# Second edge stage of a four-layer graph kernel: softmax chain over seven steps, ring of 19 groups, neighbour table made once

## Chip, cores and metric
One NeuronCore of a Trainium2 chip. The metric is the device time of one execution in microseconds, as the median of several.

## The reference
Four graph layers, one after the other, on 3125 nodes of 64 features and 53125 edges (`src`, `dst`), sorted by `dst`; each layer adds to `x` what it makes of `h = relu(layernorm(x))`. The change is in the second, a graph attention layer with 4 heads of 64 features and a self-loop on each node:

```python
xw = (x @ W).reshape(n, H, C)                      # H = 4, C = 64
alpha = a_src_n[src2] + a_dst_n[dst2] + a_edge     # an edge and head each; src2, dst2 with self-loops
alpha = jnp.where(alpha >= 0, alpha, NEG_SLOPE * alpha)
amax = jax.ops.segment_max(alpha, dst2, num_segments=n)
ae = jnp.exp(alpha - amax[dst2])
attn = ae / jax.ops.segment_sum(ae, dst2, num_segments=n)[dst2]
agg = jax.ops.segment_sum(xw[src2] * attn[:, :, None], dst2, num_segments=n)
proj = (agg.reshape(n, H * C) + bias) @ Wp + bp     # then elu, a residual, a layer norm
```

## The kernel before, in words
Edges stand in 416 tiles of 128, the edge on the partition. Four tiles are a group (104 groups), eight groups a chunk of 32 tiles (13 chunks). The program is one block of instruction streams after another, all engines meeting between two blocks: setup, then for each layer a node block, an edge block and a fold.

**Setup** (L166 on). SyncE loads indices and weights, VectorE makes `dloc` and (L227) `dr_b`, each edge's place in the window of its tile, which goes to DRAM as `DL`.

**Node block of layer 2** (to L910). It makes a table `T1` in DRAM with one row of 324 numbers a node: 256 of `h @ W @ Wp`, 4 logits of the source, 64 of `h`. The 260 first also stay in SBUF as `ytab`, a view of the big accumulator's planes `acc[:, 1:3]` (125 partitions, 25 nodes in each); they are what the self-loops need later. SyncE stores them by seven DMAs (L836).

**Edge block of layer 2** (L977 to L1390), all unrolled, in steps x = 0, 1, ...; each engine goes through the same steps with its part:
- GpSimd gathers group g's rows of `T1` into a ring `ga` of RG = 14 groups by four indirect DMAs (L985); a group's room is free when TensorE has summed it (L982, L983).
- SyncE loads places `dl`, windows `win` of the destination table (24 bf16 columns, a number split in three) and, once a chunk, `drow`, the destinations in row form.
- ScalarE makes `oneT` (`places(x)`, L1019, L1021) and `one` (`one_hots`, L1028, L1032), copies loop weights (L1039), takes the exponents (L1044) and copies the finished weights of a chunk to SBUF (`back_on_edges`, L1052).
- TensorE: `logits(x)`, four matmuls of 24 columns (L1077) into one of two half banks; `sums` of group x - SCATTER (L1089, and L1098 for the node whose edges go over a chunk's end); small transposes and matmuls of the softmax.
- VectorE: the softmax of a chunk c, with its maxima and sums over equal destinations, first in rows of a transposed form (scans, L1242, L1243, ...), then over the 32 tiles (L1251 ...). `half_logits` (L1194) adds the three parts of four groups' logits; `logits(c)` at x % 8 = 0 (L1210 to L1217), `tops` also at 0 (L1235 to L1243, ends with L1222), `highest` (L1250 to L1261) and `sums_of_rows` (L1268 to L1270, L1222) at 1, `weights` (L1279 to L1294) and `carried` (L1300 to L1308) at 2, `hold` at 4 (L1313, L1314), `turn` at 5 (L1320), `settle` at 6 (L1328, L1330). In every step it also weighs a group, x - WEIGH with WEIGH = 11 (`weigh`: L1344, L1346, L1350), and adds the sums of group x - 12 to the accumulator at four starts read from memory into registers (`add_sums`: L1354, then L1360 four times).

`k.link` marks an instruction's end on a semaphore and lets the engine's next one wait for it; `k.mark` only marks it. The order of VectorE's step is written out by hand:

```python
if x % CG == 0 and soft: logits(c)
if x % CG == 1 and soft: highest(c)
if x % CG == 2 and soft: weights(c)
if 0 <= x - WEIGH < G:   weigh(x - WEIGH)
if x % CG == 0 and soft: tops(c)
if x % CG == 1 and soft: sums_of_rows(c)
if x % CG == 2 and soft: carried(c)
```

**Fold of layer 2** (L1403 on). In seven rounds of four nodes a partition: TensorE transposes the accumulator (L1410), VectorE adds (L1435, L1437), GpSimd multiplies `ytab` by the loops' weights (L1419), VectorE reduces it over the heads (L1429) and adds (L1430). Elu and layer norm follow when all rounds are done (L1444 on).

Of the kernel before, what the change touches and what calls it, by code (L numbers as in the profile page):

```python
# [92 lines left out]
def build(nc, A, out):  # L93
    with ExitStack() as ctx:
# [61 lines left out]
        DL = dram("DL", [1, EP], BF16)  # L156

# [3 lines left out]
        l_zero, l_d, l_dl = sem("l_zero"), sem("l_d"), sem("l_dl")  # L161
# [3 lines left out]
        dr_b = tmp("dr_b", [NT // GT, GT, W], BF16)  # L165
        with nc.Block() as block:  # L166
            @block.sync
            def _(sp):
# [18 lines left out]
                sp.dma_start(wre[REL:REL + 16, D:D + 4], v16[:]).then_inc(l_dl, 16)  # L187
                sp.wait_ge(l_dl, 32)
# [20 lines left out]
            def _(dve):  # L209
# [17 lines left out]
                c.mark(dve.tensor_tensor(dr_b[:], dr_f[:], dr_f[:, :, 0:1].to_broadcast([NT // GT, GT, W]), ALU.subtract))  # L227

# [171 lines left out]
        with nc.Block() as block:  # L400
# [21 lines left out]
            def _(act):  # L422
# [9 lines left out]
                act.wait_ge(e0_ones, 2)  # L432
                each_group(act, messages)
# [376 lines left out]
        with nc.Block() as block:  # L810
# [76 lines left out]
            def _(pe):  # L887
# [27 lines left out]
        G = NT // GT  # L915
        CT = 32
        CG = CT // GT
        NC = NT // CT
        RG = 14
        WEIGH = CG + 3  # L920
# [7 lines left out]
         e1_rv, e1_rh, e1_ab, e1_B, e1_ex, e1_wy, e1_ms, e1_ml, e1_S, e1_spec, e1_fix, e1_fold, e1_half, e1_exs, e1_hT, e1_own, e1_acc) = [  # L928
            sem("e1_" + x) for x in
            ("rows", "set", "oa", "one", "ta", "oT", "P", "c", "al", "T", "top", "r1", "x", "e", "f0", "sum", "r2",  # L930
             "rv", "rh", "ab", "B", "ex", "wy", "ms", "ml", "S", "spec", "fix", "fold", "half", "exs", "hT", "own", "acc")]
        HALF = CT // 2
        ga = tmp("ga1", [128, RG * GT, GW])
# [9 lines left out]
        drow = tmp("drow", [128, 2, 128], I32)  # L943
        same = tmp("same", [128, 129])
        gap = tmp("gap", [128, 129])
# [4 lines left out]
        lgt = tmp("lgt", [128, 8, CT])  # L950
# [21 lines left out]
        ring = lambda g: g % RG * GT  # L972
# [4 lines left out]
        with nc.Block() as block:  # L977
            @block.gpsimd
            def _(pool):
                for g in range(G):  # L980
# [3 lines left out]
                    for t in range(GT):  # L984
                        pool.indirect_dma_start(ga[:, ring(g) + t, :], None, T1, bass.IndirectOffsetOnAxis(  # L985
                            ap=src_i[:, g * GT + t:g * GT + t + 1], axis=0)).then_inc(e1_g[g % RG], 16)
# [26 lines left out]
            def _(act):  # L1013
# [39 lines left out]

                act.wait_ge(e1_set, 2)
                for x in range(G + SCATTER + 1):
# [3 lines left out]
                    if x % CG == 1 and 0 <= c < NC:  # L1059
                        exponents(c)  # L1060
                    if 0 <= x - WEIGH < G:
                        one_hots(x - WEIGH)
                    if x % CG == 2 and 0 <= c < NC:
                        back_on_edges(c)
                    if 0 <= x - WEIGH < G:
                        loop_weights(x - WEIGH)

            @block.tensor
            def _(pe):
                def logits(g):  # L1070
                    pe.wait_ge(e1_oT, g + 1)
                    pe.wait_ge(e1_w[g % UG], (g // UG + 1) * 64)
                    half, tiles = divmod(g * GT, HALF)
                    if tiles == 0 and half >= 2:
                        pe.wait_ge(e1_half, half - 1)
                    for t in range(GT):
                        last = pe.matmul(bank[half % 2][:, (tiles + t) * 24:(tiles + t + 1) * 24], oneT[:, g % 2, t * W:(t + 1) * W],  # L1077
                                         win[:, g % UG * GT + t, :], start=True, stop=True)
                    last.then_inc(e1_P, 1)

                def sums(g):
# [14 lines left out]
                    for t in range(GT):  # L1096
                        at = g % CG * GT + t
                        last = pe.matmul(part_of(c), exs[:, c % 2, at::CT], ga[:, ring(g) + t, TW:GW], start=at == 0, stop=at == CT - 1)  # L1098
# [37 lines left out]
                for x in range(G + SCATTER + 1):  # L1136
                    c = x // CG - 1
                    soft = 0 <= c < NC
                    if x < G:
                        logits(x)  # L1140
                    if x % CG == 0 and soft:
# [3 lines left out]
                    if x % CG == 2 and soft:  # L1145
                        sums_in_rows(c)
                    if 0 <= x - SCATTER < G:
# [1069 lines left out]
```

## Time and profile before
| | us |
|---|---|
| median of 3 runs (lowest, highest) | 3517.68 (3505.01, 3533.71) |
| the profiled execution, its time | 3510.65 |
| its span, first to last instruction | 3508.9 |
| busy in the span: TensorE, VectorE, GpSimd, ScalarE | 2551.3, 2280.8, 1789.0, 1062.1 |

Line numbers are those of the kernel before. A timeline row has the start, the length, the engine, the line, the operation, what it writes and reads, and in brackets how long its engine stood idle before it and who ended that. PE is TensorE, PEld its weight loads, DVE VectorE, ACT ScalarE, POOL GpSimd, SP SyncE.

### The profile page before, as it was taken

What the parts mean: (1) busy time and instruction counts of PE and PEld (TensorE: products, weight loads), DVE (VectorE), ACT (ScalarE), POOL (GpSimd) and SP (SyncE); (2) the same over time, 40 slices, a digit from 0 to 9 for tenths busy, and PEclk for the clock granted to TensorE, in tenths of its full rate; (3) what the DMA queues carried; (4) which work ended last, traced back from release to release, by engine and by line L of the source; (5) the groups of instructions that cost most, each with busy time, mean ns of one, the idle gap of its engine ahead of it and who ended that gap; (6) DMA issues with size and microseconds to landing.
All of it is one profiled execution on the core that took longest, in us unless ns stands there. A gap on an engine that the chain in (4) does not pass through costs nothing. (4 is left out here: it accounts for less than half of the span.)

```text
span 3508.9 us, 58176 instructions
## 1 busy us (share of the span) xinstructions
PE 2551.3 (73%) x14132; PEld 2166.8 (62%) x14132; DVE 2280.8 (65%) x5044; ACT 1062.1 (30%) x2723; POOL 1789.0 (51%) x1813
## 2 busy tenths in 40 slices
PE   3778777514554444357777765999999999999986
PEld 2778776413443333245555544888888888888872
DVE  3555555337887887855556542677777777777775
ACT  1111111134554564111111101344444344443441
POOL 2777776066666663157777723444444344443400
PEclk7776777556555666589999967999999999999985
DMA  2443443265554552035445517988888888888830
GB/s 64 93 87 84 87 87 64 46 161 131 132 123 125 132 124 72 2 110 157 153 153 161 158 63 177 203 204 197 197 201 199 200 198 190 193 200 198 195 92 9
DMA packets 433884, 475.50 MB, mean 136 GB/s; under 512 B 200837, under 2 KB 304648, under 8 KB 433712
## 3 DMA queue, kind: packets, MB, share of 16 engines
q1 hardware_dynamic: 358832, 295.60, 35.9%
q0 software_dynamic: 59904, 123.64, 15.2%
q10 hardware_dynamic: 14976, 54.53, 4.5%
q14 instruction: 134, 1.10, 0.1%
q8 instruction: 38, 0.62, 0.1%
HBM read 408.18 MB, written 65.34 MB: 135 GB/s over the span
## 5 line engine op out<-in xcount | busy, mean ns | idle before, releaser
L1960 PE MATMUL psum<-ckv,z 128*128 128x256 f32 x4160 | 969.7, 384 | 0.0
L1960 PEld LDWEIGHTS psum<-ckv,z 128*128 128x128 f32 x4160 | 767.9, 191 | 98.5
L1823 POOL DMA_INDIRECT ga<-XX,src_i x416 | 398.1, 957 | 449.7 <-PE psum L1941 307.0
L985 POOL DMA_INDIRECT ga<-T,src_i x416 | 431.4, 1037 | 302.3 <-issue 112.5
L275 POOL DMA_INDIRECT ga<-T,src_i x416 | 401.3, 965 | 151.7 <-issue 124.4
L275 POOL DMA_INDIRECT ga<-TA,src_i x416 | 412.4, 991 | 126.7 <-issue 126.7
L2009 DVE TENSOR_TENSOR z<-psum,shb 128x2560 f32<-128x2560 f32 x104 | 293.7, 2824 | 125.8 <-PE psum L1941 78.5
L455 PE MATMUL psum<-wre,re 128*128 128x68 f32 x832 | 213.4, 349 | 142.1 <-DVE oneT L331 82.6
L1816 POOL TENSOR_TENSOR acc<-acc,wkv 128x512 f32<-128x512 f32 x104 | 114.3, 1099 | 332.7 <-DMA wkv<-WKV 316.4
L455 PEld LDWEIGHTS psum<-wre,re 128*128 128x128 f32 x832 | 173.4, 258 | 162.9 <-issue 153.9
L2050 DVE TENSOR_TENSOR acc<-acc,psum 128x256 f32 x416 | 175.4, 422 | 120.2 <-PE psum L1932 90.9
L1864 ACT ACTIVATE acc<-psum 128x512 f32<-128x512 f32 x104 | 62.1, 597 | 577.5 <-PE psum L1950 577.4
L1628 DVE TENSOR_TENSOR acc<-acc,psum 64x128 f32 x416 | 118.6, 285 | 154.9 <-PE psum L1583 110.6
L1583 PE MATMUL psum<-one,ga 128*128 128x128 f32 x832 | 128.1, 301 | 119.7 <-DMA ga<-T,src_i 107.0
L1596 ACT ACTIVATE hid<-psum,b1kv 128x512 f32<-128x512 f32 x104 | 71.5, 687 | 462.6 <-PE psum L1575 462.6
L1567 PEld LDWEIGHTS psum<-w2kv,hid 128*128 128x128 f32 x832 | 165.3, 199 | 74.1 <-issue 55.5
L1089 PE MATMUL psum<-HT 128*68 128x128 f32 x832 | 184.9, 397 | 32.9 <-DVE HT L1350 31.0
L456 PE MATMUL psum<-win,oneT 128*128 128x64 f32 x832 | 208.8, 343 | 0.0
L1583 PEld LDWEIGHTS psum<-one,ga 128*128 128x128 f32 x832 | 112.2, 207 | 150.9 <-issue 140.5
L1567 PE MATMUL psum<-w2kv,hid 128*128 128x256 f32 x832 | 203.7, 389 | 0.0
L1931 PE MATMUL psum<-one,edge_a 128*128 128x128 f32 x832 | 161.3, 304 | 53.8 <-DVE acc L2050 43.2
L428 ACT ACTIVATE msg<-pre 128x256 f32<-128x256 f32 x104 | 43.5, 419 | 505.7 <-DVE pre L481 483.0
(349 smaller groups left out, 4862.8 us busy)
## 6 DMA issues: line engine op xcount, KB each, us to landing
shb<-in_ea SPq DMA_DIRECT2D x104, 640.0 KB
WKV<-wkvo ACTq DMA_DIRECT2D x104, 512.0 KB
shb<-in_ea SPq DMA_DIRECT2D x104, 512.0 KB
wkv<-WKV SPq DMA_DIRECT2D x104, 512.0 KB
dl<-DL SPq DMA_DIRECT2D x312, 128.0 KB, 3.5
acc<-QW SPq DMA_DIRECT2D x416, 64.0 KB
win<-TB SPq DMA_DIRECT2D x416, 32.0 KB
ga<-T,src_i POOLq DMA_INDIRECT x832
```

Of the source, the lines that this page charges most:

```text
L275: pool.indirect_dma_start(o, None, table, bass.IndirectOffsetOnAxis(ap=src_i[:, g * GT + t:g * GT + t + 1], axis=0)).then_inc(s_g[k], 16)
L455: pe.matmul(P[:, o:o + D + 4], re[:, k % ER, t * W:(t + 1) * W], wre[:], start=True, stop=False)
L456: last = pe.matmul(P[:, o:o + D], oneT[:, k % 2, t * 128:(t + 1) * 128], win[:, k * GT + t, 0:D], start=False, stop=True)
L985: pool.indirect_dma_start(ga[:, ring(g) + t, :], None, T1, bass.IndirectOffsetOnAxis(ap=src_i[:, g * GT + t:g * GT + t + 1], axis=0)).then ...
L1089: last = pe.matmul(bank[4 + g % 2][0:D + 4, t * 128:(t + 1) * 128], msg[:, g % 2, t, :], one[:, g % OR * GT + t, :], start=True, stop=True)
L1567: last = pe.matmul(kvp(k)[:, t * 256:(t + 1) * 256], hid[:, k % 2, t * 128:(t + 1) * 128], w2kv[:], start=True, stop=True)
L1583: last = pe.matmul(bank[k % 2][:, t * 128:(t + 1) * 128], ga[:, pair:pair + 2, :].rearrange("p a f -> p (a f)"), one[:, k * GT + t, :], st ...
L1823: pool.indirect_dma_start(ga[:, (g % GR) * GT + t, :], None, XX, bass.IndirectOffsetOnAxis(ap=src_i[:, g * GT + t:g * GT + t + 1], axis=0) ...
L1931: pe.matmul(bank[6][:, o:o + 128], M3[:, k % 2, t, :], one[:, k % OR * GT + t, :], start=True, stop=True)
L1960: last = pe.matmul(kv_of(k)[:, t, :], z[:, k % 2, j, t * 128:(t + 1) * 128], ckv[:, j, :], start=(j == 0), stop=(j == NZ - 1))
L2009: dve.tensor_tensor(z[:, k % 2], bank[0][:].unsqueeze(1).to_broadcast([128, NZ, GT * W]), shb[:, k % 2], ALU.mult).then_inc(e3_z, 1)
L2050: dve.tensor_tensor(a, a, bank[6][:, (t % 2) * 256:(t % 2 + 1) * 256].rearrange("p (r n) -> p r n", r=2), ALU.add).then_inc(e3_acc, 1)
```

## The change
- The neighbour flags (is an edge's destination that of the edge before it, and the same as a penalty of 0 or -1e30) are made once in the setup by three VectorE instructions, stored in DRAM as `SGT` and loaded a chunk at a time in place of `drow`. `same` and `gap` are views of it.
- The ring has 19 groups: 14 in `ga` and 5 in `gb`, a view of `acc[:, 1:3]`, where `ytab` lay. The fold loads the loops' rows (256 columns of `T1`) again, by seven DMAs on SyncE, each before the GpSimd product of its round.
- A product and its sum come two steps later (WEIGH = 13, SCATTER = 14). The pieces of the softmax stand at x % 8 = 0 to 7, each between `weigh`, now first in the step, and `add_sums`; `settle` goes to the next step 0.
- The three parts of a logit are added by TensorE in PSUM (twelve matmuls of 8 columns), `half_logits` is gone, and `logits` reads PSUM. ScalarE copies the transposed logits to SBUF (`rows_out`), exponents and `back_on_edges` move to x % 8 = 2 and 4.
- `carried` has four small steps instead of six; the wait for their product (`ratios`) comes a step later.

```diff
+                c.link(dve.memset(rows_eq[:, :, 0:129], 1.0))
+                c.link(dve.tensor_tensor(rows_eq[:, :, 1:W], dr_f[:, :, 1:W], dr_f[:, :, 0:W - 1], ALU.is_equal))
+                c.mark(dve.tensor_scalar(rows_eq[:, :, 129:258], rows_eq[:, :, 0:129], -1.0, BIG, ALU.add, ALU.mult))
...
+                sp.wait_ge(c_dve, 15)
+                sp.dma_start(SGT.rearrange("(p t) e -> p t e", t=GT), rows_eq).then_inc(l_sg, 16)
...
-        RG = 14
-        WEIGH = CG + 3
+        RG = 19
+        RA = 14
+        WEIGH = CG + 5
         SCATTER = WEIGH + 1
...
+        ga = tmp("ga1", [128, RA * GT, GW])
+        gb = acc[:, 1:3, :].rearrange("p a n -> p (a n)")[:, 0:(RG - RA) * GT * GW].rearrange("p (t f) -> p t f", f=GW)
...
-                        sp.wait_ge(e1_top, c - 1)
+                        sp.wait_ge(e1_ab, c - 1)
                     for h in range(4):
-                        sp.dma_start(drow[h * CT:(h + 1) * CT, c % 2, :],
-                                     A["dst_rows"][c * CT:(c + 1) * CT, :]).then_inc(e1_dr[c % 2], 16)
+                        sp.dma_start(rows_sg[h * CT:(h + 1) * CT, c % 2, :], SGT[c * CT:(c + 1) * CT, :]).then_inc(e1_dr[c % 2], 16)
...
+                def rows_out(c):
+                    act.wait_ge(e1_T, c + 1)
+                    if c:
+                        act.wait_ge(e1_x, c)
+                    act.activation(lr[:].rearrange("p a e -> p (a e)"), lt[:, 0:256], ACT.Copy).then_inc(e1_lr, 1)
...
                     if x < G:
                         places(x)
-                    if x % CG == 1 and 0 <= c < NC:
-                        exponents(c)
                     if 0 <= x - WEIGH < G:
                         one_hots(x - WEIGH)
+                        loop_weights(x - WEIGH)
+                    if x % CG == 0 and 0 <= c < NC:
+                        rows_out(c)
                     if x % CG == 2 and 0 <= c < NC:
+                        exponents(c)
+                    if x % CG == 4 and 0 <= c < NC:
                         back_on_edges(c)
-                    if 0 <= x - WEIGH < G:
-                        loop_weights(x - WEIGH)
...
                     for t in range(GT):
-                        last = pe.matmul(bank[half % 2][:, (tiles + t) * 24:(tiles + t + 1) * 24], oneT[:, g % 2, t * W:(t + 1) * W],
-                                         win[:, g % UG * GT + t, :], start=True, stop=True)
+                        for q in range(3):
+                            last = pe.matmul(bank[c % 2][:, (t0 + t) * 8:(t0 + t + 1) * 8], oneT[:, g % 2, t * W:(t + 1) * W],
+                                             win[:, g % UG * GT + t, q * 8:(q + 1) * 8], start=q == 0, stop=q == 2)
...
-                    k.link(dve.tensor_tensor(same[:, 1:128], drow[:, c % 2, 1:128], drow[:, c % 2, 0:127], ALU.is_equal))
-                    k.mark(dve.tensor_scalar(gap[:, 1:128], same[:, 1:128], -1.0, BIG, ALU.add, ALU.mult))
                     k.mark(dve.tensor_scalar(gaps[:], meet[:, :, t0:t0 + CT + 1], -1.0, BIG, ALU.add, ALU.mult))
-                    dve.wait_ge(e1_T, c + 1)
-                    k.mark(dve.tensor_copy(top[:], lt[:, 0:128]))
-                    dve.wait_ge(e1_c, k.n)
-                    k.link(dve.tensor_tensor(top[:], top[:], lt[:, 128:256], ALU.max))
+                    dve.wait_ge(e1_lr, c + 1)
+                    k.link(dve.tensor_tensor(top[:], lr[:, 0, :], lr[:, 1, :], ALU.max))
...
-                    k.link(dve.tensor_tensor(tiny[:, 3:4], tiny[:, 3:4], tiny[:, 4:5], ALU.mult))
-                    k.mark(dve.tensor_tensor(rv[:, 0:1], tiny[:, 3:4], meet[:, 1, t0:t0 + 1], ALU.subtract))
-                    k.link(dve.tensor_tensor(tiny[:, 4:5], base_i[:, t0:t0 + 1], last_i[:, t0 + CT:t0 + CT + 1], ALU.is_equal))
-                    k.link(dve.tensor_tensor(rv[:, 1:2], tiny[:, 3:4], tiny[:, 4:5], ALU.mult))
+                    k.mark(dve.scalar_tensor_tensor(rv[:, 0:1], tiny[:, 3:4], tiny[:, 4:5], meet[:, 1, t0:t0 + 1], ALU.mult, ALU.subtract))
+                    k.link(dve.scalar_tensor_tensor(rv[:, 1:2], tiny[:, 3:4], tiny[:, 4:5], span[:, c:c + 1], ALU.mult, ALU.mult))
                     dve.sem_inc(e1_rv, 1)
+
+                def ratios(c):
+
                     dve.wait_ge(e1_rh, c + 1)
...
+                    if 0 <= x - WEIGH < G:
+                        weigh(x - WEIGH)
                     if x % CG == 0 and soft:
                         logits(c)
                     if x % CG == 1 and soft:
+                        tops(c)
+                    if x % CG == 2 and soft:
                         highest(c)
-                    if x % CG == 2 and soft:
+                    if x % CG == 3 and soft:
+                        sums_of_rows(c)
+                    if x % CG == 4 and soft:
                         weights(c)
...
+                    if x % CG == 5 and soft:
                         carried(c)
...
+                    if x % CG == 6 and soft:
+                        ratios(c)
+                        if c:
+                            hold(c)
+                    if x % CG == 7 and soft and c:
                         turn(c)
+                    if x % CG == 0 and 0 < c - 1 < NC:
+                        settle(c - 1)
                     if 0 <= x - SCATTER < G:
                         add_sums(x - SCATTER)
...
+                for r, (j0, n) in enumerate(rounds(NJ, 4)):
+                    sp.dma_start(ytab[:, j0:j0 + n, :], T1.rearrange("(j p) f -> p j f", p=PN)[:, j0:j0 + n, 0:HY]).then_inc(m1_l[r], 16)
...
                     pool.wait_ge(m1_la, r + 1)
+                    pool.wait_ge(m1_l[r], 16)
```

TensorE's step has `sums` right behind `logits`, and its softmax pieces at 0, 1, 3, 4, 5, 6 and 7.

## Rows read from the trace of the kernel before
**Rows 1.** Windows: stretch, length, busy PE, PEld, DVE, ACT, POOL, clock, DMA share, GB/s.
```profile
720.00:1380.00 660.00, 300.27 (x2117) 242.40 (x2118) 500.87 (x1330) 340.23 (x805) 424.44 (x410) 0.61 0.53 130
```

**Rows 2.** Waits of 720 to 1380 us: engine, line, for whom: us, times, longest.
```profile
ACT HT L1044 <- DVEq L1263: 188.8, 12, 17.2
POOL ga L985 <- PE psum L1098: 112.0, 39, 4.9
POOL ga L985 <- issue: 111.0, 364, 0.3
```

**Rows 3.** Timeline of VectorE, one chunk: start us, us, instruction [idle before].
```profile
1060.74 0.31 DVE L1217 SCALAR_TENSOR_TENSOR lg<-lg 128x128 f32<-128x128 f32 x1
1061.19 1.23 DVE L1344 TENSOR_TENSOR ga<-ga,ex 128x1024 f32<-128x1024 f32 x1
...
1063.52 0.35 DVE L1235 TENSOR_TENSOR same<-drow 128x127 f32<-128x127 int32 x1
...
1064.04 0.25 DVE L1237 TENSOR_SCALAR gaps<-meet 128x99 f32<-128x99 f32 x1
1064.21 0.28 DVE L1239 COPY top<-psum 128x128 f32<-128x128 f32 x1
...
1066.67 1.53 DVE L1360 TENSOR_TENSOR acc<-acc,psum 68x128 f32 x4 [0.69 <-DVE diag L1222]
...
1086.22 0.16 DVE L1308 COPY rho<-psum 68x2 f32<-68x2 f32 x1 [0.54 <-PE psum L1118]
...
1092.62 0.55 DVE L1194 TENSOR_REDUCE lgt<-psum 128x128 f32<-128x384 f32 x1
...
1104.31 0.42 DVE L1350 TENSOR_TENSOR HT<-ga 128x256 f32<-128x256 f32 x1
1104.87 1.53 DVE L1360 TENSOR_TENSOR acc<-acc,psum 68x128 f32 x4
1106.70 0.15 DVE L1328 TENSOR_TENSOR acc<-acc,psum 64x1 f32 x1 [0.30 <-DVE acc L1360]
...
1112.64 0.38 DVE L1210 TENSOR_TENSOR lg<-ga,lgt 128x128 f32<-128x128 f32 x1 [0.89 <-DVE lgt L1194]
```

**Rows 4.** Source line L1217: ns min/median/max, first and last start in us.
```profile
L1217 DVE SCALAR_TENSOR_TENSOR lg<-lg x13: 291/292/366, 756.4 to 1376.9; 128x128 f32<-128x128 f32 x13
```

**Rows 5.** Timeline of VectorE, first and second chunk's first logits.
```profile
755.39 0.38 DVE L1210 TENSOR_TENSOR lg<-ga,lgt 128x128 f32<-128x128 f32 x1 [15.11 <-DMA ga<-T,src_i]
...
796.23 0.44 DVE L1210 TENSOR_TENSOR lg<-ga,lgt 128x96 f32<-128x96 f32 x2 [2.82 <-DMA ga<-T,src_i]
```

**Rows 6.** Timeline of ScalarE, weights back on edges, then places.
```profile
1083.05 0.38 ACT L1052 ACTIVATE ex<-psum 128x256 f32<-128x256 f32 x1 [5.55 <-PE psum L1123]
...
1084.19 0.72 ACT L1021 ACTIVATE oneT<-oneT,ones_c 128x512 bf16<-128x512 bf16 x1
```

**Rows 7.** Timeline of TensorE, the sums and the logits of one group.
```profile
1061.64 1.92 PE L1089 MATMUL psum<-HT 128*68 128x128 f32 x8
...
1064.43 0.28 PE L1077 MATMUL psum<-win,oneT 128*128 128x24 bf16 x4
```

**Rows 8.** Timeline of the fold: its first TensorE and last small VectorE sum.
```profile
1441.14 1.06 PE L1410 MATMUL psum<-ident,acc 68*125 68x68 f32 x8 [1.04 <-PEq L977]
...
1462.57 0.23 DVE L1430 TENSOR_TENSOR m_XC<-m_XC,yl 125x64 f32<-125x64 f32 x1
```

**Rows 9.** DMA while the table with the loops' rows is stored, 684 to 709 us.
```profile
DMA packets 2550, 2.63 MB, mean 105 GB/s; under 512 B 25, under 2 KB 2550, under 8 KB 2550
...
q1 hardware_dynamic: 2550, 2.63, 33.8%
```

**Rows 10.** Windows again, 6 to 8 us, while x is loaded.
```profile
6.00:8.00 2.00, 0.00 (x0) 0.00 (x0) 2.00 (x1) 0.00 (x0) 0.00 (x0) 1.00 0.40 91
```

**Rows 11.** Timeline of VectorE: end of the setup, start of the next block.
```profile
17.13 0.69 DVE L227 TENSOR_TENSOR dr_b<-dr_f 104x512 bf16<-104x512 f32 x1
20.33 1.82 DVE L236 TENSOR_REDUCE st<-X 125x25 f32<-125x1600 f32 x1 [2.51 <-PEq L166]
```

More of the change, by code:

```diff
@@ L915, in build @@
         G = NT // GT
+        HY = 4 * D
+        TW = HY + 4
         CT = 32
@@ L942, in build @@
         pfirst = tmp("pfirst", [128, NT])
-        drow = tmp("drow", [128, 2, 128], I32)
-        same = tmp("same", [128, 129])
-        gap = tmp("gap", [128, 129])
+        rows_sg = tmp("rows_sg", [128, 2, 258])
+        span = tmp("span", [128, NC])
         gaps = tmp("gaps", [128, 3, CT + 1])
@@ L971, in build, with rows_of_group @@
         hrow = lambda v: v.rearrange("p (h t) -> p h t", h=4)
-        ring = lambda g: g % RG * GT
+        same_of = lambda c: rows_sg[:, c % 2, 0:129]
+        gap_of = lambda c: rows_sg[:, c % 2, 129:258]
+        def rows_of_group(g, a, b):
+            k = g % RG
+            return ga[:, k * GT:(k + 1) * GT, a:b] if k < RA else gb[:, (k - RA) * GT:(k - RA + 1) * GT, a:b]
         lt = bank[2]
@@ L1097, in sums @@
                         at = g % CG * GT + t
-                        last = pe.matmul(part_of(c), exs[:, c % 2, at::CT], ga[:, ring(g) + t, TW:GW], start=at == 0, stop=at == CT - 1)
+                        last = pe.matmul(part_of(c), exs[:, c % 2, at::CT], rows_of_group(g, TW, GW)[:, t, :], start=at == 0, stop=at == CT - 1)
                     last.then_inc(e1_spec, 1)
@@ L1140, in _ @@
                         logits(x)
+                    if 0 <= x - SCATTER < G:
+                        sums(x - SCATTER)
                     if x % CG == 0 and soft:
@@ L1164, in constants @@
                     k.mark(dve.memset(meet[:], 0.0))
-                    k.mark(dve.memset(same[:], 1.0))
-                    k.mark(dve.memset(gap[:], 0.0))
                     k.mark(dve.memset(sel_o[:], 0.0))
@@ L1188, in constants @@
                     dve.sem_inc(e1_set, 1)
-                def half_logits(half):
-                    dve.wait_ge(e1_P, (half + 1) * (HALF // GT))
-                    t0 = half % 2 * HALF
-                    k.link(dve.tensor_reduce(lgt[:, :, t0:t0 + HALF],
-                                             bank[half % 2][:, 0:HALF * 24].rearrange("p (t q f) -> p f t q", q=3, f=8), AX.X, ALU.add))
-                    dve.sem_inc(e1_half, 1)
                 def logits(c):
@@ L1268, in sums_of_rows @@
                     k.link(dve.tensor_tensor(top[:], wt[:, 0, :], wt[:, 1, :], ALU.add))
-                    k.link(dve.tensor_tensor_scan(scan[:, 0, :], same[:, 0:128], top[:], 0.0, ALU.mult, ALU.add))
-                    k.link(dve.tensor_tensor_scan(scan[:, 1, ::-1], same[:, 128:0:-1], top[:, ::-1], 0.0, ALU.mult, ALU.add))
+                    k.link(dve.tensor_tensor_scan(scan[:, 0, :], same_of(c)[:, 0:128], top[:], 0.0, ALU.mult, ALU.add))
+                    k.link(dve.tensor_tensor_scan(scan[:, 1, ::-1], same_of(c)[:, 128:0:-1], top[:, ::-1], 0.0, ALU.mult, ALU.add))
                     edges_of_rows()
@@ L1289, in weights @@
                     at_own_row()
-                    k.link(dve.tensor_tensor_scan(scan[:, 0, :], same[:, 0:128], top[:], ecol[:, 0:1], ALU.mult, ALU.add))
+                    k.link(dve.tensor_tensor_scan(scan[:, 0, :], same_of(c)[:, 0:128], top[:], ecol[:, 0:1], ALU.mult, ALU.add))
                     k.link(dve.tensor_tensor(ecol[:, 1:2], ecol[:, 1:2], scan[:, 0, 127:128], ALU.add))
-                    k.link(dve.tensor_tensor_scan(full[:, ::-1], gap[:, 128:0:-1], scan[:, 0, ::-1], ecol[:, 1:2], ALU.add, ALU.max))
+                    k.link(dve.tensor_tensor_scan(full[:, ::-1], gap_of(c)[:, 128:0:-1], scan[:, 0, ::-1], ecol[:, 1:2], ALU.add, ALU.max))
                     k.link(dve.reciprocal(full[:], full[:]))
```

76 lines of the change are left out of this document (35 added, 41 removed).

## The prediction
> **What bounds the kernel now.** I read the table by stretch first, to see which engine fills the second edge stage, the only long stage that the change touches. It runs from 711 us to 1441 us; between 720 and 1380 us VectorE is busy 501 of 660 us, GpSimd 424, ScalarE 340, TensorE 300 [rows 1]. Busy time alone doesn't make VectorE the bound, so the waits come next: who stands still, and for whom. The large waits are of other engines for VectorE: ScalarE 189 us for the exponents' argument; GpSimd 112 us for TensorE's sums, which follow VectorE's products [rows 2]. VectorE's own timeline settles it. Its step after a linked instruction starts 0.03 to 0.04 us behind it (L1235 to L1237 [rows 3]), and what is left of gaps is the engine's own work: register loads and semaphore waits that its sequencer handles between two instructions. So the stage is a string of VectorE instructions, and its length is that string's. The period is steady: L1217 runs once in a chunk of 32 tiles, 13 times; the seventh starts at 1060.74 us [rows 3], the last at 1376.9 us [rows 4], so 316.2 / 6 = 52.7 us a chunk.
>
> The profiled execution took 3510.65 us around a span of 3508.9 us, 7 us under the median of the three runs (3517.68). I work out a difference and put it on both.
>
> **VectorE per chunk: what goes** (start to start, linked instructions with their 0.04 us):
> - The first half reduction L1194: 0.70 us to the product that follows [rows 3].
> - The second, and the wait train ahead of L1210: 0.55 us of work and 0.89 us idle in this chunk; over all chunks the idle part is mostly 0.55, so 1.12 us as a mean. The logits now stand behind a product, whose last instruction (0.42 us) covers part of the nine waits; I leave 0.40. Gone: 0.72.
> - L1235 and L1236 (neighbour flags, now from a table): 1063.52 to 1064.04, 0.52, mean 0.49. L1239 (copy out of PSUM, now ScalarE's): its 0.31 up to the next start (from 1064.21 [rows 3]).
> - Two of six scalar steps at the end of the weights: 2 x 0.19 (such a step is 0.16 long, as L1308 [rows 3], and 0.19 with its link) less 0.04 each for the fused forms: 0.30.
> - L1308 waits 0.54 us for TensorE's round trip [rows 3]; a step later the answer is there. But the chain piece before it then ends in its own exposed register load (next paragraph), and L1308 costs 0.19 elsewhere: net 0.40.
> Sum 2.92 us.
>
> **What comes.** `add_sums` reads four window starts into registers before its first add. Behind a linked instruction this shows whole: 0.69 us idle ahead of L1360 at 1066.67. Behind a product that isn't linked only 0.14 us show (L1350 at 1104.31, 0.42 long, L1360 at 1104.87) [rows 3]. Before, four of eight steps end linked; now seven do.
> - Logits: L1217 to the product is a gap of 0.14 now, and 0.69 to the settling afterwards: +0.50 (start to start, means).
> - `settle` moves between logits and `add_sums`: both read registers, and neither hides the other. It shows 0.30 idle behind an add now [rows 3]; then 0.69 stands behind its own last instruction: +0.27.
> - `highest` and `weights` end linked and meet `add_sums` instead of a product: +0.54 and +0.55.
> - Three steps had no chain piece and paid 0.23 us more between L1350 and L1360 than a step that has one; they have one now: -0.70.
> - The ring in two parts cuts the logits' first addition into 23 pieces instead of 19: +0.05.
> Sum +1.21 us. A chunk gains 2.92 - 1.21 = 1.7 us: 51.0 instead of 52.7. I bound the gain by 1.0 (wait train uncovered) and 2.4 (fused steps and waits cheaper). Twelve chunks feel it: 20.4 us, from 12 to 29.
>
> **The ring and the start.** Chunk 0 has nothing beside it. L1210 runs at 755.39 when the gathers of 8 groups have landed, and for chunk 1 at 796.23, again behind gathers [rows 5]. By then five products and four additions of sums were done; with the products two steps later it is four and two. One product of 2.33 and two additions of 1.45 (0.20 + 3 x 0.42) move behind the wait: +5.2 us; the longer ring takes away about 1.1 us for which the 15th gather was held: +4.1. After that the ring moves nothing: VectorE waits for no gather in the steady chunks, so GpSimd's 112 us [rows 2] were slack. Bounds 0 and +8. The stage: -20.4 + 4.1 = -16.3 us.
>
> **Hidden edits.** The copy of the logits on ScalarE (as L1052, 0.38 us [rows 6]) lies in its idle time: 340 of 660 us busy. Its step stands until the logits are done, and behind it queue the places of the next group (L1021 ends them), TensorE's logits of it, and the sums that VectorE adds at the end of the next step. The tightest of these hand-overs is the one behind `weights`: transposes and copy take 1.3 us, places 1.5, logits 0.6, sums 1.9 [rows 6, 7], so 5.3 us; VectorE needs them after 0.69 + 1.45 + 0.20 + 2.33 + 0.6 + 0.69 = 5.96. It fits by 0.65 us. Twelve logit matmuls stand in place of four, which take 0.28 us together [rows 7]: 0.6 us if each adds what one does now, 2.2 if each stood alone at 0.18. The rows' loads are four per chunk as before, with 1032-byte rows, and SyncE reaches them long after the flag it now waits for. The table itself is three VectorE instructions of 508 or 516 elements in the setup (L227, of 512 elements, takes 0.69 us [rows 11]), some 1.8 us; 2 to 3 us of that stand beside a DMA that the block waits for anyway: +0.3, at most +2.
>
> **The rows of the loops.** They lay in the room that the ring takes, so the fold reads them again: 3125 rows of 1024 bytes, 3.2 MB in seven loads, issued when the block starts (1441.1 us), and its seven rounds now end at 1462.8 us with the last L1430 [rows 8]. The nearest row is the opposite way: the stores of the same table, also over 125 partitions, move 105 GB/s with 0.34 of the 16 DMA engines busy, hardly more than five [rows 9]. 3.2 MB / 105 GB/s = 30.5 us, and with 2 us to land (the setup's last store is released by L227 at 17.8 us, and the next block starts on its landing at 20.3 us [rows 11]) the last rows come at 1473.7. The round before has landed at 1472.5: product 1.9, reduction 1.9, sum 0.4, then the last small round 0.8: the fold ends at 1477.5. +14.7 us, all on the path, since VectorE's next instruction needs every round. Bounds: the input x, 125 partitions in 256-byte rows, loads at 91 GB/s [rows 10]: 35 us, +19. If the load spread over all 16 engines at the same 21 GB/s each it would be hidden but for the first round: +3.
>
> That a transfer over 125 partitions should be slow is also the rule of the Trainium skill (DMA: Bandwidth & Descriptors, section "Why a DMA increments its semaphore by 16 and not by 1"): the number of DMA engines is the largest up to 16 that divides the slowest dimension of both sides, five for 125; the stores' 0.34 agrees. The same page's table of measured loads (section "Bandwidth") has 341 GB/s for 1 MB over 128 partitions; by that the seven loads would take 9.4 us and cost 3 us in all.
>
> **Sum.** -16.3 + 14.7 + 0.3 = -1.3 us. The profiled execution would be at 3509, the median at 3516.5. About what can be told from no change here is 1%, 35 us: no measurable difference.
>
> **Rivals.**
> 1. *The reload is hidden* (a read spreads where the store does not). For it: gathers of 1296-byte rows reach far more in the same stage. Against: x is a load and goes at 91 GB/s. Time: -16.3 + 3 + 0.3, 3504.5.
> 2. *The hand-over to ScalarE and TensorE takes VectorE's place as the bound; slower.* Place: behind `weights`, `highest` and the logits, where ScalarE stands until VectorE is done and only then makes the places. Point: 0.65 us of slack; over it every 0.1 us costs 1.2 us. If twelve matmuls and twelve weight loads run one after another (0.18 + 0.11 each, 3.5 us against 0.6), the step behind `weights` is 2.2 us late and the one behind `highest` 0.8: +3.0 a chunk, +36 us, with my sum 3552. Against: in the trace four such matmuls overlap to 0.28 us. A half of it (1.5 us a chunk) gives 3534.
> 3. *The gathers were the bound after all* and the ring of 19 frees them. For: GpSimd's 112 us. Then a chunk takes what 32 gathers take, 1.04 + 0.30 us each [rows 1, 2]: 42.7 us, -10 a chunk, 3397. Against: no gather wait on VectorE once chunk 1 is in.
>
> **Chances.** My sum within some 8 us: 0.62. Rival 1: 0.12. Rival 2: 0.18, of which 0.06 over 1%. Rival 3: 0.03. The rest, 0.05, is split. So faster 0.05, same 0.88, slower 0.07. Bounds: stage -29 to -4, reload +3 to +19, setup 0 to +2, and a median of a few runs scatters (3505 to 3534 here): 3494 to 3540.
>
> **What would show it.** L1217's successor every 51 us, not 52.7; 0.69 us idle ahead of seven L1360 groups a chunk; GpSimd's wait for TensorE much smaller with no gain from it; seven loads at about 105 GB/s in the fold, GpSimd's products there 4.9 us apart, the rounds of the fold over at 36 us after its start instead of 22. I am wrong if VectorE waits for TensorE ahead of its additions in the steady chunks, if the period is under 49.5 or over 53 us, or if the loads of the fold land within 20 us.

## Result and the profile after

| | before, us | after, us |
|---|---|---|
| median (lowest, highest) of 15 and 15 runs on one chip | 3513.05 (3497.22, 3533.71) | 3529.13 (3522.00, 3537.72) |
| span of the profiled execution | 3508.9 | 3529.2 |
| second edge stage, to the fold | 729.8 | 715.4 |
| fold of layer 2 | 44.2 | 55.5 |
| edge block of layer 4 | 1306.2 | 1333.8 |
| edge blocks of layers 1 and 3 | 549.8, 535.0 | 548.8, 531.9 |

Ratio 1.0037, 95% interval 1.0021 to 1.0053: slower by 0.4%, under the 1% that I called a change, but not nothing. The lower part of the table is the length of each block in the profiled execution, from its first to its last instruction or DMA issue. The two blocks that I had worked out moved by -14.4 and +11.3 us, as forecast in sign and size. The 27.6 us that make the result are in the edge block of layer 4, of which the change touches no line.

The same windows as [rows 1], and the source row that answers to [rows 4], of the kernel after:

```profile
720.00:1380.00 660.00, 328.20 (x2969) 265.78 (x2969) 486.29 (x1281) 347.24 (x832) 427.14 (x409) 0.61 0.54 131
```
```profile
L1236 DVE SCALAR_TENSOR_TENSOR lg<-lg x13: 291/291/322, 755.2 to 1355.2; 128x128 f32<-128x128 f32 x13
```
The second of the thirteen starts at 796.0 us: (1355.2 - 796.0) / 11 = 50.8 us a chunk. GpSimd's long wait of [rows 2] is mostly gone, and nothing came of it:

```profile
POOL ga L1002 <- PE psum L1122: 38.7, 11, 4.7
```
VectorE's timeline of one chunk, against [rows 3]. In brackets is the idle time before a row:

```profile
1253.93 0.29 DVE L1236 SCALAR_TENSOR_TENSOR lg<-lg 128x128 f32<-128x128 f32 x1
1254.91 0.15 DVE L1344 TENSOR_TENSOR acc<-acc,psum 64x1 f32 x1 [0.69 <-DVE lg L1236]
...
1255.89 1.53 DVE L1376 TENSOR_TENSOR acc<-acc,psum 68x128 f32 x4 [0.59 <-DVE acc L1346]
...
1261.97 1.53 DVE L1376 TENSOR_TENSOR acc<-acc,psum 68x128 f32 x4 [0.69 <-DVE diag L1241]
...
1269.94 1.53 DVE L1376 TENSOR_TENSOR acc<-acc,psum 68x128 f32 x4 [0.68 <-DVE HT L1276]
```
The register loads ahead of the sums (L1376, L1360 before) stand open behind the piece of the chain, as worked out. No row of VectorE's waits in the steady chunks names TensorE or a DMA.

The fold: SyncE's seven loads, GpSimd's products that wait for them, and the last sum.

```profile
1425.51 22.43 SPq L1435 DMA_DIRECT2D m_y<-T  x7
...
1440.69 1.90 POOL L1443 TENSOR_TENSOR m_y<-m_y,la 125x1024 f32<-125x1024 f32 x1 [2.33 <-DMA m_y<-T]
...
1444.93 1.90 POOL L1443 TENSOR_TENSOR m_y<-m_y,la 125x1024 f32<-125x1024 f32 x1 [2.35 <-DMA m_y<-T]
...
1458.29 0.22 DVE L1454 TENSOR_TENSOR m_XC<-m_XC,yl 125x64 f32<-125x64 f32 x1
```
GpSimd's products start 4.24 us apart, one for each load of 512,000 bytes: 121 GB/s. The rounds are over 33 us after the start.

Now the block that I left out. TensorE is busy there 94% of the time. First the kernel before (window, then TensorE's two largest groups, then VectorE's largest), then the one after:

```profile
2139.00:3445.00 1306.00, 1230.93 (x6890) 1089.58 (x6890) 950.82 (x1902) 525.64 (x1353) 512.35 (x520) 0.97 0.81 188
```
```profile
L1960 PE MATMUL psum<-ckv,z 128*128 128x256 f32 x4160 | 969.7, 384 | 0.0
L1931 PE MATMUL psum<-one,edge_a 128*128 128x128 f32 x832 | 161.3, 304 | 53.8 <-DVE acc L2050 43.2 <-DVE edge_a L2033 10.6
```
```profile
2132.00:3465.00 1333.00, 1242.59 (x6890) 1100.11 (x6890) 953.32 (x1901) 525.49 (x1353) 514.09 (x520) 0.96 0.79 185
```
```profile
L1984 PE MATMUL psum<-ckv,z 128*128 128x256 f32 x4160 | 980.7, 387 | 0.0
L1955 PE MATMUL psum<-one,edge_a 128*128 128x128 f32 x832 | 161.9, 305 | 67.6 <-DVE acc L2074 57.0 <-DVE edge_a L2057 10.6
```
Same code, same counts. TensorE waits 13.8 us longer for VectorE's additions (43.2, 57.0), and its largest group of matmuls takes 11.0 us more. These waits come once a turn of the loop over groups, when VectorE goes back from the loop's end to its head. One such turn, before and after:

```profile
2523.97 0.69 DVE L2033 TENSOR_TENSOR edge_a<-vw,ex 128x512 f32<-128x512 f32 x1 [0.30 <-DVE exb L683]
...
2527.91 2.82 DVE L2009 TENSOR_TENSOR z<-psum,shb 128x2560 f32<-128x2560 f32 x1 [3.25 <-issue]
```
```profile
2517.84 0.69 DVE L2057 TENSOR_TENSOR edge_a<-vw,ex 128x512 f32<-128x512 f32 x1 [0.65 <-DVE exb L691]
...
2522.53 2.83 DVE L2033 TENSOR_TENSOR z<-psum,shb 128x2560 f32<-128x2560 f32 x1 [4.00 <-issue]
```
From the end of the branch to the next instruction VectorE is silent for 2.95 us before and 3.74 us after, as a mean over eleven turns. In that silence the trace has transfers of the instruction queue, 8192 bytes each: one before, two after, at each of the eleven turns. The two rows below are the DMA view of such a silence (2524.13 to 2527.12 us before, 2518.01 to 2521.74 us after):

```profile
q14 instruction: 1, 0.01, 1.1%
```
```profile
q14 instruction: 2, 0.02, 2.4%
```
An entry of the compiled stream has 64 bytes, so a fetch brings 128. VectorE's compiled stream has 4078 entries before and 3979 after: the change took 99 away, all ahead of this loop. Counted in the program, the loop's head is instruction 3376 before (48 over a multiple of 128) and 3276 after (76 over). The compiled stream has 68 and 69 further entries ahead of the loop, so there the heads are 3444 and 3345, 116 and 17 over a multiple of 128. I go on with the program's count. Only how far two kernels' heads lie apart means something, since no trace shows where the stream begins in the memory that it is fetched from.

### The profile page after: what moved, and what is told of

It reads as the page before. It is cut to its first block and busy times, and to the rows that moved or that the text cites. A ratio compares the mean times of both kernels' runs of the same rounds, so it can differ in the third digit from the quotient of the medians.

```text
span 3529.2 us, 59775 instructions
## 1 busy us (share of the span) xinstructions
PE 2574.1 (73%) x14964; PEld 2186.6 (62%) x14964; DVE 2258.4 (64%) x4959; ACT 1064.0 (30%) x2736; POOL 1788.1 (51%) x1813
## 3 DMA queue, kind: packets, MB, share of 16 engines
q0 software_dynamic: 59904, 123.64, 15.4%
## 5 line engine op out<-in xcount | busy, mean ns | idle before, releaser
L1984 PE MATMUL psum<-ckv,z 128*128 128x256 f32 x4160 | 980.7, 387 | 0.0
L1984 PEld LDWEIGHTS psum<-ckv,z 128*128 128x128 f32 x4160 | 775.7, 193 | 101.4
L282 POOL DMA_INDIRECT ga<-T,src_i x416 | 396.1, 952 | 151.7 <-issue 124.0
L1002 POOL DMA_INDIRECT ga<-T,src_i x316 | 329.9, 1044 | 207.7 <-issue 92.6
L1955 PEld LDWEIGHTS psum<-one,edge_a 128*128 128x128 f32 x832 | 147.4, 201 | 88.9 <-DVE acc L2074 64.2
```

The lines of the kernel that those rows point to most:

```text
L282: pool.indirect_dma_start(o, None, table, bass.IndirectOffsetOnAxis(ap=src_i[:, g * GT + t:g * GT + t + 1], axis=0)).then_inc(s_g[k], 16)
L1002: pool.indirect_dma_start(rows_of_group(g, 0, GW)[:, t, :], None, T1, bass.IndirectOffsetOnAxis(ap=src_i[:, g * GT + t:g * GT + t + 1], ax ...
L1955: pe.matmul(bank[6][:, o:o + 128], M3[:, k % 2, t, :], one[:, k % OR * GT + t, :], start=True, stop=True)
L1984: last = pe.matmul(kv_of(k)[:, t, :], z[:, k % 2, j, t * 128:(t + 1) * 128], ckv[:, j, :], start=(j == 0), stop=(j == NZ - 1))
```

## The experiments

Two theories: **C**, the place of the loop in VectorE's stream makes the second fetch and the longer block; **L** or **R**, something else of the change does (DRAM tables that moved, SBUF, other engines). The runs fell on four other chips, where the edge blocks of layers 1 and 3 take some 150 and 110 us more; I compare within a chip as far as I can. Every ratio has the kernel before on the same chip under it. Of traces, the first chip has none of the changed kernel as it is, the second none of the kernel before, the third neither; there a block is set beside the nearest run's.

**First chip.** The kernel before, for its trace:

> The kernel before, unchanged, for a second profile of it. The changed kernel is 28 us slower in the edge block of layer 4, whose program text it doesn't touch: 1306.2 us before, 1333.8 after, with VectorE silent for 3.0 us after each of the eleven branches back to the loop's head before and 3.8 us after. Theory N (that block's time differs from execution to execution by that much): this profile shows a block of anything from 1306 to 1334 us. Theories L (place of the tables in DRAM) and C (place of the loops' code): 1306 us within 3, and 3.0 us of silence again.

Measured: one fetch at a turn, silence 3.63 us, layer-4 block 1332.8 us. The 1306 and 3.0 us of the expectation were figures of the chip of the result, so this run alone can't decide between the theories. `layout_only` adds the table and a store to the kernel before:

```diff
         DL = dram("DL", [1, EP], BF16)
+        SGT = dram("SGT", [NT, 258])
...
+                sp.dma_start(SGT[0:128, 0:256], zero[:]).then_inc(l_zero, 16)
```


> The kernel before, with the DRAM table SGT declared where the changed kernel declares it, and filled in part with zeros by one store in the setup, so that all later tables in DRAM lie 430 KB further on; nothing reads it. Theory L: the edge block of layer 4 takes about 1334 us and the whole is slower by 20 to 28 us. Theory C: nothing moves, 1306 us and the time of before within 5 us. Theory N: no pattern.

Measured: ratio 0.9996 (0.9973 to 1.0019), block 1325.1 us, one fetch. L, which wanted a longer block and 20 to 28 us more, falls. With nothing changed in the loop's place the block is 7.7 us shorter than in `ctrl_before`; single traces scatter by that much. `pad99` is the changed kernel with 99 instructions put back:

```diff
+                for n in range(99):
+                    dve.memset(filler[:, n:n + 1], 0.0)
```


> The changed kernel, with 99 VectorE instructions on one column each (memset) at the end of the node block of layer 3, where VectorE waits for a store anyway; VectorE's code of the later blocks then stands where it stood before the change. Theory C in its VectorE form: silence after each branch back to 3.0 us from 3.8, the edge block of layer 4 shorter by 9 us (eleven times 0.8) up to the whole 28 us, and the kernel faster than the changed one by that. Theory L: 1334 us still, total as the changed kernel plus at most 6 us. Edge block of layer 2 and its fold as in the changed kernel, 715 and 55.5 us.

`hoist` is the changed kernel with the register loads of the sums and of the settling between the first and the second product's instruction:

```diff
                     dve.tensor_tensor(y, y, w.unsqueeze(3)...).then_inc(e1_wy, 1)
+                    if load:
+                        load()
```


> The changed kernel, with the register loads of add_sums and settle moved to stand between the first two instructions of the step's product, where VectorE works 1.2 us on the first. My prediction says that in seven of eight steps such a load shows as 0.69 us idle behind a linked instruction, twice in step 0. If that is right: 0.55 us less in eight places a chunk, 4.4 us of 50.8; period 46.4 us unless the hand-over to ScalarE and TensorE behind the weights (0.65 us of slack worked out) or behind the logits now ends last, then up to 48; edge block of layer 2 shorter by 36 to 55 us. If the 0.69 us were a wait for TensorE's sums, nothing moves. The fold and the edge block of layer 4 as in the changed kernel (the number of VectorE's instructions is the same but for one).

Measured: `pad99` one fetch, block 1332.6, ratio 1.0029 (1.0011 to 1.0047); `hoist` two fetches, block 1349.5, ratio 1.0002 (0.9982 to 1.0023). The block follows the loop's place: 16.9 us between the two. But `pad99`, with one fetch and the layer-4 block of the kernel before, is still 0.3% slower than that kernel. Against `ctrl_before` layer 2's stage takes 7.8 us more (792.2, 784.4), the fold 10.6 (55.3, 44.7) and, by the filler, layer 3's node block 1.7 (19.1, 17.4); layer 1's edge block gives 8.7 back (698.1, 706.8). The hidden loads gained less than expected: 0.31 us idle ahead of a sum, not 0.69, and chunks of 48.0 us, but others of up to 55.6 us, and a mean of 51.5 against 52.3 in `pad99`, where 46.4 to 48 had been expected. In the long ones VectorE, ScalarE and GpSimd all stand still for some 4 us; I did not find out why.

**Second chip.** The effect switched on in the kernel before, and a version with several repairs:

> The changed kernel itself, beside the others of this call on one chip. Theory C (the place of VectorE's layer-4 loop in its instruction stream): two instruction fetches at each of 11 turns, VectorE silent 0.7 to 0.9 us longer at a turn than in the kernel before, the layer-4 edge block 15 to 30 us longer than that of the kernel before. Ratio to the kernel before 1.002 to 1.006.

> The kernel before with 28 one-column memsets on VectorE at the end of its part of layer 2's node block, where it stands idle; nothing of the change is in it. They move the layer-4 loop of VectorE from instruction 3376 to 3404 of its stream, as far from a multiple of 128 (76) as in the changed kernel (3276). Theory C: this alone makes two instruction fetches at a turn, the silence 0.7 to 0.9 us longer, and the layer-4 edge block 15 to 30 us longer; ratio to the kernel before 1.004 to 1.009, all of it in that block. Rival R (the longer block comes from something that the change does, in SBUF, DRAM or the other engines' streams): no difference in that block over 4 us, ratio 0.999 to 1.001.

```diff
-                    sp.dma_start(ytab[:, j0:j0 + n, :], T1...[:, j0:j0 + n, 0:HY]).then_inc(m1_l[r], 16)
+                    for a, b in ((0, 112), (112, PN)):
+                        sp.dma_start(ytab[a:b, j0:j0 + n, :], T1...[a:b, j0:j0 + n, 0:HY]).then_inc(m1_l[r], 16)
```


> The changed kernel with two edits in separate blocks. (1) The fold's loads cut at partition 112: 112 and 13 partitions. If the number of DMA engines is the largest divisor up to 16 of the slowest dimension, 112 go over 16 engines (8 rows each over 14 or 16) and 13 over 13, so the loads end within 12 us instead of 29, and the fold's block is 45 to 49 us long instead of 55.5. If the reload is bound by something else (its 1024-byte packets, the reads from DRAM), the block stays at 53 to 57. (2) 52 memsets move the layer-4 loop of VectorE to instruction 3328, a multiple of 128. Theory C: one fetch at a turn, at most as long a silence as in the kernel before, the layer-4 edge block 15 to 30 us shorter than that of after_again. Rival R: that block as in after_again. Ratio to the kernel before by C and the divisor rule: 0.993 to 0.998; by the rivals 1.001 to 1.005.

> The changed kernel with the fold's loads cut at 112 partitions, the register loads of the starts moved ahead of the second product's instruction, and 98 memsets that put the layer-4 loop at instruction 3375 or 3376, where the kernel before has it. By theory C one fetch at a turn and the layer-4 block of the kernel before; by the divisor rule the fold at 45 to 49 us; and the register loads hidden, a period of 48 to 49 us in place of 50.8, 22 to 34 us shorter over 12 chunks. Sum against the kernel before: -15 - 28 + 3 = -40 us, ratio 0.986 to 0.992. If theory C is wrong the layer-4 block stays long and the ratio is 0.993 to 0.998.

| | ratio to before (95%) | fetches | layer-4 block | fold | first, second logits after the stage's start |
|---|---|---|---|---|---|
| after_again | 1.0079 (1.0055, 1.0103) | 2 | 1339.5 | 55.2 | 111.9, 145.9 |
| before_pad28 | 1.0050 (1.0035, 1.0065) | 2 | 1343.0 | 44.2 | 84.8, 125.8 |
| split_pad52 | 1.0026 (1.0011, 1.0042) | 1 | 1332.6 | 47.1 | 110.6, 143.7 |
| best98 | 0.9987 (0.9971, 1.0004) | 1 | 1331.6 | 47.0 | 110.8, 145.5 |

28 idle memsets alone make the kernel before 0.5% slower. The block of `split_pad52` is only 7 us shorter than `after_again`'s, not 15 to 30, and its ratio misses the expected 0.993 to 0.998. The fold's answer is clear: cut at partition 112 the loads use 88.9% of the 16 DMA engines in the 12 us from 1623 to 1635, and the fold loses 8 of its 11 us. Uncut, in the kernel after, they use 26.2% in the 35 us from 1420 to 1455, and 32.1%, about five engines of 16, from 1427 on. The DMA queue's row of the two stretches, after and then `split_pad52`:

```profile
q1 hardware_dynamic: 3160, 3.20, 26.2%
```
```profile
q1 hardware_dynamic: 2829, 2.75, 88.9%
```
`best98` fell short of its -40 us, and `after_again` was worse than where the result was measured. The last column shows a large part of why: with the ring of 19 the second chunk's logits come 18 to 20 us later than in `before_pad28`. On the chip of the result it was 86.3 us before and 86.1 after. The first run on the third chip tries that.

**Third chip.** The late gathers, the short ring, and the register loads by themselves:

```diff
                         pool.wait_ge(e1_ms, g - RG + 1)
+                    elif g == RA:
+                        pool.wait_ge(e1_P, CG)
```


> The changed kernel, but GpSimd issues the gathers of groups 14 to 18 only when TensorE has the logits of the first eight groups; nothing else differs. On the chip of after_again VectorE waited 105 us for its first logits where the kernel before waited 56.5 us, and SyncE's loads of windows stood in their queue behind 19 groups of gathers. Theory S (the longer ring starves the loads of places and windows at the start, on a chip whose transfers are slow): the first wait of VectorE (L1230's place) is 60 to 85 us instead of 105, and the second edge stage 12 to 25 us shorter than after_again's 783.6 us; period unchanged. If this chip's transfers are fast (first edge stage near 550 us), no difference over 4 us. Rival: the first wait stays at 100 us or more on a slow chip (it is set by something other than the gathers of groups 14 to 18).

> The changed kernel with the ring of 14 groups, so that the loops' rows stay in SBUF and the fold has no reload; schedule and table as in the changed kernel. With products and sums two steps later, group g + 14 is gathered only after the sums of g in step g + 14, while its chunk's logits may want it in the next step. If the longer ring is needed for the later products: VectorE waits for gathers 2 to 6 us in every chunk, period 53 to 57 us instead of 50.8, the second edge stage 25 to 70 us longer. If it is not needed: period 50.5 to 51.5 and no such wait. Either way the fold is 44 us long, 11 us under the changed kernel's, and the layer-4 loop stands at instruction 3271 or 3272 (71 or 72 over a multiple of 128). Ratio to the kernel before: 1.005 to 1.018 if needed, 0.998 to 1.003 if not.

> The kernel before with only the register loads of the sums' starts (and of the settling's start) moved ahead of the second product's instruction; nothing of the change. Idle time ahead of the additions goes from 0.69 to about 0.31 us where a linked instruction precedes them (four of eight steps) and from 0.14 to about 0 elsewhere: 1.5 to 2.2 us a chunk, period 50.7 to 51.3 where it was 52.7, as much as the whole change gains in this stage and without its reload. The layer-4 loop moves by one instruction (3377, 49 over a multiple of 128): one fetch at a turn, block unchanged. Ratio 0.993 to 0.996. Rival: the loads only move the wait to the second or third product's instruction: period over 52, ratio 0.998 to 1.002.

> best98 with the late gathers of groups 14 to 18. Theory S on a slow chip: the second edge stage 12 to 25 us under best98's 773.8 us, ratio to the kernel before 0.991 to 0.996; on a fast chip the ratio is 0.985 to 0.992, from the fold, the hidden register loads and the loop at its old place. Rival: as best98, 0.997 to 1.0004.

`late` has the changed kernel's place of the loop, two fetches, and a layer-4 block of 1339.1 us. Its first logits came at 86.0 us, their wait was 79.0 us, but the second chunk's came 51.8 us later where `after_again` had 34.0, with 17.2 us idle at the first maxima. Second logits at 137.8 us, the stage 783.4 us against 783.6 on the other chip: theory S holds for the first wait, its gain of 12 to 25 us is not there. Ratio 1.0022 (1.0002 to 1.0042).

`ring14`: ratio 1.0061 (1.0040 to 1.0081), the second edge stage 824.6 us, a chunk 56.9 us. VectorE's largest wait from 1000 to 1560 us, ten chunks:

```profile
DVE lg L1230 <- DMA ga<-T,src_i: 59.7, 10, 6.5
```
6.0 us a chunk, so the ring of 19 is needed, by the products that the change itself moved. Its loop (72 over) has one fetch and a block of 1324.7 us.

`before_hoist`: 0.9933 (0.9910 to 0.9956), one fetch, shortest chunks 49.9 us where the kernel before has 52.4 or 52.5 in each of its traces. Its ratio is as expected, its period is not: 52.6 us in the mean, not 50.7 to 51.3. There is no trace of the kernel before from this chip; on the first and fourth its mean is 53.8 and 55.1 us. `best_late`: 0.9916 (0.9888 to 0.9943), block 1331.6, fold 47.0; the stage of 771.5 us is 2 us under `best98`'s on the other chip, not 12 to 25. Both are faster than the kernel before, which the changed kernel was on no chip (1.0017 to 1.0079), and their intervals overlap: moved register loads in the old kernel bring nearly what the repaired change does, without ring, table or reload. `best_late` has these moved loads too, so what the change itself adds to them the runs don't show.

**Fourth chip.** The decisive table, change or not, loop at 47 or 48, or at 76:

> The kernel before, unchanged, for a trace from the same chip as the three that follow. One fetch at a turn of VectorE's layer-4 loop. All theories: its layer-4 edge block is the measure for the others.

> The changed kernel, unchanged. Theory C: two fetches at a turn, the layer-4 edge block 10 to 28 us longer than before_side's; the second edge stage's period 1.5 to 2.5 us a chunk shorter; ratio to the kernel before 1.002 to 1.008.

> The changed kernel with 99 one-column memsets at the end of VectorE's part of layer 2's node block, where it stands idle for 24 us, so that the layer-4 loop stands where the kernel before has it (3375 or 3376). Theory C: one fetch at a turn, the layer-4 edge block within 5 us of before_side's and 8 to 28 us shorter than after_side's, every other block as in after_side; median 8 to 28 us under after_side's. Rival R (something else of the change makes that block longer): block and median as after_side's, within 5 us.

> The kernel before with 28 memsets in the same idle place (loop at 3404, 76 over a multiple of 128). Theory C: two fetches at a turn, the layer-4 edge block 8 to 28 us longer than before_side's and within 5 us of after_side's. Rival R: as before_side's, within 4 us.

| | ratio (95%) | median | fetches | silence at a turn | layer-4 block |
|---|---|---|---|---|---|
| before_side | measure | 3874.5 | 1 | 3.62 | 1336.0 |
| after_pad99_idle | 0.9988 (0.9969, 1.0007) | 3871.1 | 1 | 3.72 | 1332.0 |
| before_pad28_side | 1.0040 (1.0024, 1.0056) | 3889.9 | 2 | 4.78 | 1346.0 |
| after_side | 1.0017 (0.9999, 1.0035) | 3882.8 | 2 | 4.59 | 1346.4 |

TensorE's sums in the layer-4 block, in the table's order:

```profile
L1931 PE MATMUL psum<-one,edge_a 128*128 128x128 f32 x832 | 162.7, 306 | 63.8 <-DVE acc L2050 53.2 <-DVE edge_a L2033 10.6
```
```profile
L1958 PE MATMUL psum<-one,edge_a 128*128 128x128 f32 x832 | 161.4, 304 | 63.6 <-DVE acc L2077 52.4 <-DVE edge_a L2060 10.6 <-issue 0.5
```
```profile
L1934 PE MATMUL psum<-one,edge_a 128*128 128x128 f32 x832 | 164.1, 308 | 74.6 <-DVE acc L2053 63.6 <-DVE edge_a L2036 11.0
```
```profile
L1955 PE MATMUL psum<-one,edge_a 128*128 128x128 f32 x832 | 164.2, 308 | 75.2 <-DVE acc L2074 64.6 <-DVE edge_a L2057 10.6
```
The wait for VectorE's additions is 53.2 and 52.4 us with one fetch, 63.6 and 64.6 with two, whether the change is in or not. The place alone costs 10 us in the kernel before and 14 us in the changed one; the medians differ by 15.4 and 11.7 us. Between chips single traces of this block scatter by up to 11 us with the loop in the same place (1325.1, 1336.0). Still the sixteen traces of the four chips part cleanly: 1324.7 to 1336.0 us in the ten with one fetch, 1339.1 to 1349.5 us in the six with two. Theory C holds and R falls.

## Why the prediction was wrong

**The step that failed** is the "Sum": -16.3 + 14.7 + 0.3. It took every block that the change doesn't touch as unchanged, and I bounded setup, stage and fold but never the layer-4 block. No term was there for what 99 fewer instructions do to a loop behind them. With the loop at its old place the changed kernel is at 0.9988 on the fourth chip, the "no difference, slightly faster" of the forecast. On the first chip (`pad99`) it is at 1.0029, so that part of the forecast, too, holds on one chip and not on another.

Not all of the 27.6 us is shown to be this. By the four runs the place is worth 10 to 14 us of the block, and on the chip of the result TensorE's longer wait is 13.8. Another 11.0 us are the matmuls of L1960, 384 ns before and 387 after, at a granted clock of 0.97 and 0.96; 2.8 us are neither. The same matmuls take 385 to 387 ns in each of the sixteen traces of the experiments, with one fetch or two, so the change isn't seen to make it; it is the profiled execution of before that stands alone. The profiles differ by 20.3 us, the medians by 16.1. The medians are the better measure: they moved by 17.4 us against the forecast (+16.1, not -1.3), and the place alone moved medians by 11.7 and 15.4 us on the fourth chip and by 17.4 on the second (`before_pad28`). By that estimate it is most of the miss. It was not measured on the chip of the result, and what is left of the gap is not settled.

**Point by point.**
- *VectorE's string bounds the stage*: right. Its idle time in the steady chunks is that of its own register loads, and it waits for nobody else's work.
- *Period 52.7 to 51.0*: 50.8.
- The stage's -14.4 against -16.3 hides two errors that cancel. *Start +4.1*: the second logits stand at 86.3 and 86.1 us of the stage, so -0.2. What I had left out is the end: from the last logits to the end of the stage 63.9 us before and 70.1 after, +6.2, for a product and its sum now come two steps later and nothing stands beside the last ones. With 11 x -1.85 = -20.4 that is the whole. On the four other chips the start does cost: second logits 128.6 us into the stage in `before_side`, 145.6 in `after_side`. I had bounded it at +8 from one trace. That the loads of places and windows stand behind a longer ring's gathers fits `late`'s first wait, no more. Nor is it shown that transfers are slow there, as some expectations have it: a packet of the hardware queue q1 takes 56.2 ns in the mean in `before` and 57.7 in `before_side`. The whole stage took 798.9 and 790.1 us on the fourth chip without the change (`before_side`, `before_pad28_side`), 790.8 and 792.8 with it (`after_side`, `after_pad99_idle`), so its gain isn't seen there.
- *Hidden register loads*: right that they stand behind linked instructions, at 0.69. I took them as given; the cheapest gain of the study was to move them.
- *Reload +14.7*: +11.3. The mis-sized term is the rate: 105 GB/s from the opposite direction, 121 measured. By the divisor rule of the Trainium skill (DMA: Bandwidth & Descriptors, "Why a DMA increments its semaphore by 16 and not by 1") 125 partitions get five engines. The runs agree: 32.1% of 16 engines are about five, and cut into 112 and 13 the fold lost 8 us. The 341 GB/s of the Trainium skill's same page (section "Bandwidth") is measured over 128 partitions and was no guide to 125.
- *Rival 1*, the reload hidden at +3: false as it stands, true once the loads are cut (fold 47.1 against 44.2, +2.9). *Rival 2*, TensorE and ScalarE late behind `weights`: no such wait. *Rival 3*, gathers as the bound: false, though `ring14` shows that the new order would be bound by them without the longer ring.

## What to carry over

Where a change adds or removes instructions of an engine, look at every later loop of that engine whose turns already show a silence and a fetch: the turn can cost more or less by the loop's place, and with eleven turns beside a busy TensorE this was 0.3 to 0.5% of the kernel, on the fourth chip more than the rest of the change together. Before calling such a result the edit's own, pad the stream in an idle place and measure again. And ahead of a rebuild of a schedule, read the small idle times in front of its commonest instruction: register loads moved behind a long instruction gave 0.7%, on one chip.

## What the runs showed that I had not expected

- One fetch in the silence at a turn with the loop's head 0, 47, 48 or 72 instructions over a multiple of 128, two at 76 and 77; about 1 us more silence with two (3.62 and 3.72 against 4.59 and 4.78 us). In the compiled stream these are 68, 115, 116 and 12 with one fetch, 15, 17 and 18 with two. Why the bound lies there the runs don't show.
- VectorE's loops of layers 1 and 3, of 195 and 161 instructions, turn without a fetch and without such a silence (0.2 us); the layer-4 loop has 397. Where between 195 and 397 it begins no run shows.
- The same kernel takes 3513 us on one chip and 3829 to 3875 us on the four others, some 260 of the 320 to 360 us in the edge blocks of layers 1 and 3. A term for the start of a stage, read from one chip, did not hold on another.
